# An adaLN transformer block with routed experts: token list built by one-hot matmuls, second expert row fetched by an accumulating transfer

## What is computed

```python
h = _layernorm(x) * (1 + ca) + sa
x = x + ga * linear_attention(h)            # 16 heads of 32, relu on q and k
h = _layernorm(x) * (1 + cb) + sb
x = x + gb * ffn(h)

# ffn: X is 4096 x 512, 8 experts, 2 per token
scores = sigmoid(X @ gate_w.T)
_, idx = top_k(scores + router_bias, 2)
w = scores[idx] / sum(scores[idx])
y_e = (silu(X @ W1[e]) * (X @ W3[e])) @ W2[e]        # inner width 352
out = sum_k w_k * y_idx_k + (silu(X @ sw1.T) * (X @ sw3.T)) @ sw2.T   # shared, width 704
```

## Time and profile before

| | |
|---|---|
| median of 3 runs | 1439.48 us |
| profiled execution | 1446.23 us, span 1444.4 us |
| mean granted TensorE clock | 0.934 |
| TensorE busy | 1249.8 us (87%) |
| VectorE busy | 661.2 us (46%) |
| GpSimd busy | 479.6 us (33%) |
| ScalarE busy | 415.7 us (29%) |

### The profile page before, as it was taken

The page is one execution under the profiler, slowest core; times in us unless marked ns, Lnnn a source line. Parts: engine busy times, 40 slices in busy tenths (PEclk is TensorE's granted clock), DMA queues, the critical chain, the costliest instruction groups (busy, mean ns, idle before and its releaser), DMA issues.

```text
span 1444.4 us, 25152 instructions
## 1 busy us (share of the span) xinstructions
PE 1249.8 (87%) x8990; PEld 788.6 (55%) x8990; DVE 661.2 (46%) x1376; ACT 415.7 (29%) x869; POOL 479.6 (33%) x460
## 2 busy tenths in 40 slices
PE   6997998998997989662488699999999999988896
PEld 2645665665665556440256456556565666565563
DVE  4555777777866556551145311111111111145764
ACT  2432443434433324230133212222222222211121
POOL 1213555555643322067400101111111111067661
PEclk9998999999998999885599899999999999989998
DMA  5724786987878577142135345655556555477773
GB/s 183 226 44 116 171 196 162 210 213 168 204 190 239 148 193 206 55 110 63 50 114 151 116 105 129 134 127 139 133 132 132 132 132 132 110 235 231 214 237 118
DMA packets 270067, 220.33 MB, mean 153 GB/s; under 512 B 190640, under 2 KB 203184, under 8 KB 269436
## 3 DMA queue, kind: packets, MB, share of 16 engines
q1 hardware_dynamic: 242424, 159.65, 43.8%
q0 software_dynamic: 12848, 35.47, 9.3%
q10 hardware_dynamic: 14680, 23.62, 5.7%
HBM read 117.29 MB, written 57.61 MB: 121 GB/s over the span
## 4 chain that ended last, share of the span: by engine, by line
PE 52%; issue 13%; DVE 10%; DMA 10%; POOL 9%; ACT 3%; SPq 3%; ACTq 1%; DVEq 0%; POOLq 0%
PE ps_o L75 6%; PE ps_vs L75 5%; PE ps_o L76 5%; PE ps_o L77 5%; PE ps_vs L76 5%; PE ps_vs L77 5%; DMA xt<-g 4%; PE ps_kh L75 2%; PE ps_kh L76 2%; PE ps_kh L77 2%; POOL ol L394 2%; DMA wp_raw<-in_wproj_t 2%; POOL h L381 1%; POOL xg L389 1%; PE ps_qh L75 1%
## 5 line engine op out<-in xcount | busy, mean ns | idle before, releaser
L455 POOL DMA_INDIRECT g<-h_d,slot_tab x71 | 67.1, 945 | 472.4 <-DMA xt<-g 352.1
L75 PE MATMUL ps_o<-w_all,xt 128*128 x568 | 179.6, 316 | 19.4 <-DMA xt<-g 19.3
L76 PE MATMUL ps_o<-w_all,xt 128*128 x568 | 179.5, 316 | 0.0
L77 PE MATMUL ps_o<-w_all,xt 128*128 x568 | 179.2, 316 | 0.0
L861 DVE SCALAR_TENSOR_TENSOR a<-ps_o,a 128x352 f32<-128x352 f32 x71 | 37.2, 524 | 183.3 <-PE ps_o L77 183.3
L866 DVE TENSOR_TENSOR at<-ps_y,at 128x384 f16<-128x384 f32 x71 | 39.6, 557 | 176.3 <-ACT at L1105 176.3
L75 PE MATMUL ps_kh<-s_ht,sh 128*128 128x256 f16 x256 | 79.5, 310 | 43.3 <-DVE s_act L620 30.4
L1110 ACT ACTIVATE y<-ps_vs,slot_tab 128x512 f32<-128x512 f32 x71 | 48.8, 687 | 230.5 <-PE ps_vs L77 230.5
L75 PE MATMUL ps_qh<-ht,wqkv 128*128 128x128 f16 x512 | 90.4, 223 | 2.5 <-DVE wqkv L613 2.5
L370 POOL TENSOR_TENSOR h<-cen,rows_f 128x512 f32<-128x512 f32 x32 | 40.6, 1268 | 154.4 <-ACT cen L904 143.0
L76 PE MATMUL ps_qh<-ht,wqkv 128*128 128x128 f16 x512 | 90.4, 223 | 0.0
(11 more groups left out here) (225 smaller groups left out, 3267.5 us busy)
## 6 DMA issues: line engine op xcount, KB each, us to landing
y_d<-y SPq DMA_DIRECT2D x71, 256.0 KB, 3.4
w_stage<-in_w_d ACTq DMA_DIRECT2D x64, 176.0 KB
xb<-in_x SPq DMA_DIRECT2D x32, 256.0 KB, 3.3
xr<-in_x SPq DMA_DIRECT2D x32, 256.0 KB, 4.2
x_d<-x SPq DMA_DIRECT2D x32, 256.0 KB, 3.5
h_d<-hl SPq DMA_DIRECT2D x32, 256.0 KB, 2.7
h2t_d<-h2t SPq DMA_DIRECT2D x32, 256.0 KB, 3.7
s_ht<-h2t_d SPq DMA_DIRECT2D x32, 256.0 KB
```

Of the source, the lines that this page charges most:

```text
L75: nc.tensor.matmul(out, lh, rh, start=first, stop=False, skip_group_check=True)
L76: nc.tensor.matmul(out, lh, rl, start=False, stop=False, skip_group_check=True)
L77: return nc.tensor.matmul(out, ll, rh, start=False, stop=last, skip_group_check=True)
L455: pool.indirect_dma_start(m.g[:, t % 2, :], None, m.h2_d, bass.IndirectOffsetOnAxis(ap=m.slot_tab[:, t, 0:1], axis=0)).then_inc(m.gathered ...
```

## The change

**Choosing.** `find_top` and `find_index` are replaced by `pick`: for each of the two ranks a maximum over all tiles at once, a comparison, and the lowest expert number of those equal. `add_runs` uses one scan in place of eight. The routing is done in steps 22 to 25.

**The list.** No table in DRAM. A token's slot is split into lane (slot mod 128) and tile (slot / 128). For each of 64 pairs of token tile and rank, VectorE makes two one-hot operands: `lane_is` (128x128) and `tile_is` (128 x 71 x 4), the latter times four values: tile number, token in the tile, and high and low part of the weight. TensorE adds up their products in one PSUM bank. Six pairs per step in steps 26 to 36; at step 37 `list_tokens` turns the sum into token numbers and weights.

**Weights.** From piece 22 on the low part is GpSimd's. As its subtraction can't scale, ScalarE scales the staged piece in place in a second pass. The 66 pieces are spread evenly over the steps up to the experts.

**Order.** EARLY is 8: the early stage is steps 22 to 47, and 48 steps run after the experts. **Combine.** `y_sum` is gone; the second row of a token is fetched with `compute_op=ALU.add` onto the first, once that has landed, three tiles ahead. GpSimd's constants grow by a few small instructions. The names of routing now take the room of the last two experts, so ScalarE waits for `listed` at piece 66.

```diff
-EARLY = 10
+EARLY = 8
...
+PAIRS = TOP * TILES
+PAIR_RING = 8
+PAIRS_PER_STEP = 6
+PAIRS_FROM = TAIL_STEPS + 4
+PICKED = 4
...
-    first = TAIL_STEPS + 2 * (q - TAIL_STEPS)
-    return range(min(first, E * WP), min(first + 2, E * WP))
+    left, steps, i = E * WP - TAIL_STEPS, EARLY_STEPS - TAIL_STEPS, q - TAIL_STEPS
+    return range(TAIL_STEPS + left * i // steps, TAIL_STEPS + left * (i + 1) // steps)
...
+def pair_turn(q):
+    first = PAIRS_PER_STEP * (q - PAIRS_FROM)
+    return range(min(max(first, 0), PAIRS), min(max(first + PAIRS_PER_STEP, 0), PAIRS))
...
-    for j in range(2):
-        sp.wait_ge(m.scattered[j], 16 * TILES)
-    sp.dma_start(m.slot_tab[:, :, :], m.table.rearrange("(p t) o -> p t o", p=P)).then_inc(m.table_loaded, 16)
...
-    pool.wait_ge(m.slots_ready, 1)
-    pool.wait_ge(m.table_stored, 16)
-    for t in range(TILES):
-        for k in range(TOP):
-            pool.indirect_dma_start(m.table, bass.IndirectOffsetOnAxis(ap=m.entry[:, k, t:t + 1], axis=0),
-                                    m.tab_src[:, k, t, :], None).then_inc(m.scattered[k], 16)
...
+    def w_low(p):
+        _, dst, rows, cols = w_piece(m, p)
+        pool.wait_ge(m.w_hi, p + 1)
+        pool.wait_ge(m.w_scaled, p - TAIL_STEPS + 1)
+        pool.tensor_tensor(dst[:, 1, :], m.w_stage[0:rows, p % W_RING, 0:cols], dst[:, 0, :], ALU.subtract).then_inc(m.w_lo, 1)
+
+    pool.wait_ge(m.w_lo, TAIL_STEPS)
+    for p in range(TAIL_STEPS, E * WP):
+        w_low(p)
...
     def fetch(i):
         if i < len(order):
             r = i % YB
+            at_least(pool, m.y_loaded[i % Y_RING], 32 * (i // Y_RING))
             if i >= YB:
                 before = order[i - YB]
                 pool.wait_ge(m.c_added if before < 2 * EARLY else m.s_t1_done, before + 1)
-            for k in range(TOP):
-                pool.indirect_dma_start(m.yb[:, r, k, :], None, m.y_d,
-                                        bass.IndirectOffsetOnAxis(ap=m.slot[:, k, order[i]:order[i] + 1], axis=0)).then_inc(m.y_loaded[i % Y_RING], 16)
-
-    def y_sum(i):
+            pool.indirect_dma_start(m.yb[:, r, 0, :], None, m.y_d,
+                                    bass.IndirectOffsetOnAxis(ap=m.slot[:, 0, order[i]:order[i] + 1], axis=0)).then_inc(m.y_loaded[i % Y_RING], 16)
+
+    def fetch_onto(i):
         r = i % YB
-        pool.wait_ge(m.y_loaded[i % Y_RING], 2 * ring_use(i, Y_RING))
-        pool.tensor_tensor(m.yb[:, r, 0, :], m.yb[:, r, 0, :], m.yb[:, r, 1, :], ALU.add).then_inc(m.y_summed, 1)
-
-    for i in range(2):
+        pool.wait_ge(m.y_loaded[i % Y_RING], 2 * ring_use(i, Y_RING) - 16)
+        pool.indirect_dma_start(m.yb[:, r, 0, :], None, m.y_d,
+                                bass.IndirectOffsetOnAxis(ap=m.slot[:, 1, order[i]:order[i] + 1], axis=0),
+                                compute_op=ALU.add).then_inc(m.y_loaded[i % Y_RING], 16)
+
+    for i in range(3):
         fetch(i)
     for i in range(len(order)):
-        fetch(i + 2)
-        y_sum(i)
+        fetch_onto(i)
+        fetch(i + 3)
...
+    def pick():
         v.wait_ge(m.scores_ready, 1)
+        v.wait_ge(m.r_consts, PICKED)
         step(v.tensor_tensor(m.sel[:, :, :], m.scores[:, :, :], m.bias[:, :].unsqueeze(1).to_broadcast([P, TILES, E]), ALU.add))
-        for t in range(TILES):
-            v.max(m.top[:, t, :], m.sel[:, t, :]).then_inc(m.r_step, 1)
-        steps += TILES
-        v.wait_ge(m.r_step, steps)
-
-    def find_index():
-        nonlocal steps
-        for t in range(TILES):
-            v.max_index(m.index[:, t, :], m.top[:, t, :], m.sel[:, t, :]).then_inc(m.r_step, 1)
-        steps += TILES
-        v.wait_ge(m.r_step, steps)
+        for k in range(TOP):
+            step(v.reduce_max(m.best[:, :], m.sel[:, :, :], AX.X))
+            step(v.tensor_tensor(m.cand[:, :, :], m.sel[:, :, :], m.best[:, :].unsqueeze(2).to_broadcast([P, TILES, E]), ALU.is_equal))
+            step(v.scalar_tensor_tensor(out=m.cand[:, :, :], in0=m.cand[:, :, :], scalar=-float(E),
+                                        in1=m.expert_far[:, :].unsqueeze(1).to_broadcast([P, TILES, E]), op0=ALU.mult, op1=ALU.add))
+            step(v.tensor_reduce(m.best[:, :], m.cand[:, :, :], AX.X, ALU.min))
+            step(v.tensor_tensor(m.choice[:, k, :, :], m.expert_no[:, :].unsqueeze(1).to_broadcast([P, TILES, E]),
+                                 m.best[:, :].unsqueeze(2).to_broadcast([P, TILES, E]), ALU.is_equal))
+            if k == 0:
+                step(v.scalar_tensor_tensor(out=m.sel[:, :, :], in0=m.choice[:, k, :, :], scalar=-BIG, in1=m.sel[:, :, :],
+                                            op0=ALU.mult, op1=ALU.add))
+        v.tensor_tensor(m.both[:, :, :], m.choice[:, 0, :, :], m.choice[:, 1, :, :], ALU.add).then_inc(m.both_ready, 1)
...
+    def pair(n):
+        t, k, r = n // TOP, n % TOP, n % PAIR_RING
+        at_least(v, m.pair_used, n - PAIR_RING + 1)
+        v.tensor_scalar(m.lane_is[:, r, :], m.lane_no[:, :], m.part[:, 0, k, t:t + 1], None, ALU.is_equal).then_inc(m.pair_ready, 1)
+        v.scalar_tensor_tensor(out=m.tile_is[:, r, :, :], in0=m.tile_no[:, :, :], scalar=m.part[:, 1, k, t:t + 1],
+                               in1=m.values[:, k, t, :].unsqueeze(1).to_broadcast([P, SLOT_TILES, 4]),
+                               op0=ALU.is_equal, op1=ALU.mult).then_inc(m.pair_ready, 1)
...
+    def list_tokens():
+        v.wait_ge(m.pair_used, PAIRS)
+        step(v.tensor_copy(m.listing[:, :, :], m.ps_list))
+        step(v.scalar_tensor_tensor(out=m.tokenf[:, :], in0=m.listing[:, :, 0], scalar=float(P), in1=m.listing[:, :, 1],
+                                    op0=ALU.mult, op1=ALU.add))
+        step(v.tensor_copy(m.slot_token[:, :], m.tokenf[:, :]))
+        step(v.tensor_tensor(m.tokenf[:, :], m.listing[:, :, 2], m.listing[:, :, 3], ALU.add))
+        v.tensor_scalar(m.slot_weight[:, :], m.tokenf[:, :], 1.0 / SCALE ** 2, None, ALU.mult).then_inc(m.listed, 1)
...
-    beside = {TAIL_STEPS: (find_top,), TAIL_STEPS + 1: (find_index,), TAIL_STEPS + 2: (weigh,),
-              TAIL_STEPS + 3: (add_runs,), TAIL_STEPS + 4: (place,), TAIL_STEPS + 5: (name_tiles,)}
+        step(v.tensor_copy(m.eid[:, :], m.eidf[:, :]))
+
+    beside = {TAIL_STEPS: (pick,), TAIL_STEPS + 1: (weigh,), TAIL_STEPS + 2: (add_runs,), TAIL_STEPS + 3: (place, name_tiles)}
     sum_logits()
     for q in range(TAIL_STEPS, EARLY_STEPS):
         multiply(q)
+        for n in pair_turn(q):
+            pair(n)
         low(q - 1)
         for work in beside.get(q, ()):
             work()
         if down_due(q):
             add(q // SH_TILES - 1)
-        for p in w_turn(q):
-            w_low(p)
+        if q == LIST_STEP:
+            list_tokens()
...
         act.wait_ge(m.w_loaded[p % W_RING], ring_use(p, W_RING))
-        act.activation(dst[:, 0, :], m.w_stage[0:rows, p % W_RING, 0:cols], ACT.Copy, scale=SCALE).then_inc(m.w_hi, 1)
+        staged = m.w_stage[0:rows, p % W_RING, 0:cols]
+        act.activation(dst[:, 0, :], staged, ACT.Copy, scale=SCALE).then_inc(m.w_hi, 1)
+        if p >= TAIL_STEPS:
+            act.wait_ge(m.w_hi, p + 1)
+            act.activation(staged, staged, ACT.Copy, scale=SCALE).then_inc(m.w_scaled, 1)
...
-        if q == TAIL_STEPS + 3:
+        if q == TAIL_STEPS + 1:
...
+        for n in pair_turn(q):
+            pe.wait_ge(m.pair_ready, 2 * n + 2)
+            nc.tensor.matmul(m.ps_list.rearrange("p t n -> p (t n)"), m.lane_is[:, n % PAIR_RING, :], m.tile_is[:, n % PAIR_RING, :, :].rearrange("p t n -> p (t n)"),
+                             start=n == 0, stop=n == PAIRS - 1, skip_group_check=True).then_inc(m.pair_used, 1)
```

More of the change, by code:

```diff
@@ L408, in gpsimd_program @@
         if s == 0:
-            step(pool.memset(m.zero[:, :], 0))
             step(pool.memset(m.ident[:, :], 0.0))
@@ L412, in gpsimd_program @@
                                     base=0, pattern=[[-1, P]], channel_multiplier=1))
-            step(pool.iota(m.token[:, :], [[P, TILES]], base=0, channel_multiplier=1))
-            step(pool.tensor_copy(m.tab_src[:, :, :, 0], m.token[:, :].unsqueeze(1).to_broadcast([P, TOP, TILES])))
         if s == 2:
@@ L639, in add @@
             v.wait_ge(m.sy_done, i + 1)
-            if n < EARLY and n in (0, 8):
-                v.wait_ge(m.s_gb_loaded, 48 if n == 0 else 64)
+            if n == 0:
+                v.wait_ge(m.s_gb_loaded, 48)
             v.wait_ge(m.act_done, SH_TILES * (n + 1))
@@ L782, in find_index @@
-    def find_index():
-        nonlocal steps
-        for t in range(TILES):
-            v.max_index(m.index[:, t, :], m.top[:, t, :], m.sel[:, t, :]).then_inc(m.r_step, 1)
-        steps += TILES
-        v.wait_ge(m.r_step, steps)
-    def weigh():
-        v.wait_ge(m.r_consts, 4)
-        for k in range(TOP):
-            step(v.tensor_copy(m.indexf[:, k, :], m.index[:, :, k]))
-            step(v.tensor_tensor(m.choice[:, k, :, :], m.expert_no[:, :].unsqueeze(1).to_broadcast([P, TILES, E]),
```

(17 more changed lines are left out.)

107 lines of the change are left out of this document (58 added, 49 removed).

## The result

The changed kernel takes 1473.85 us (median of four runs, 1473.1 to 1477.98). The kernel before, run beside it, takes 1438.87 us (four runs, 1435.37 to 1442.59). The ratio is 1.0249 with an interval of 1.0216 to 1.0281: slower by 35 us. The forecast was 1473.0, from 1430 to 1510.

The account below looks back on a forecast made before the run. It took weight pieces to pace undisturbed early chunks, beside a scatter stall; TensorE bounds the experts. From 1446.2 us, -11 before the experts and +45 in the combine stage gave 1480, less 6.7 for the median 1473; range 1430 to 1510.

Parts of the forecast that it names:

- the 14 for the clock: Early stage after 606 us: 14 us added for slower matmuls, an eighth to a half of 47 us being 6 to 24.
- Step 1: Early stage, 648.8 to 710.6 us: the 64 table scatters and the stall beside them go, -55.6 us.
- Rival B: Early stage: something other than the scatters holds the engines, so the stall stays, +55.6 us, 1529; chance 0.06.
- Step 2: Routing: fewer instructions save some 3 us; the down product of step 26 releases ScalarE at 606 instead of 609.1.
- Step 3: Weight pieces from 22 on: ScalarE's second pass and GpSimd's subtraction in series, 2.41 us narrow, 3.02 wide.
- Step 4: Steps 26 to 36: pairs take TensorE's lead, 7.7 us a step; first two chunks 60.4 and 53.6 us.
- Step 5: Combine stage: two more chunks add 53.4 us, less 4.5 and 4 from dropping GpSimd's sums; net +45.
- full relief: Combine stage: the lower bound of the net cost of moving twelve steps there, +39 us.
- Step 6: Combine stage: 32 accumulating transfers replace 32 sums; 0 us for the first tile.
- Rival C: Combine stage: accumulating transfers above 6.7 us each outlast a chunk; at 8 us, about 1505; chance 0.08.
- A: Steps 26 to 36: pairs cost TensorE no lead, pieces alone set the pace; 1434 to 1440 us; chance 0.15.
- D: Early stage: half of A, pair step near 6.5 us, pieces 2.4, first expert matmul near 783; 1440; chance 0.09.

Follow-up runs that it names:

- x6: Kernel before with the accumulating fetch and each residual row tile of the combine stage loaded one turn later: 1425.48 us, ratio 0.9903.
- x3: Kernel after with weight low parts back on VectorE, no second ScalarE pass, and TensorE's pair matmuls one step later: 1421.95 us, ratio 0.988.
- x4: Kernel after with ten chunks ahead of the experts instead of eight: 1474.17 us, ratio 1.0238 to the kernel before.
- x5: Kernel after with low parts on VectorE, pair matmuls one step later and ten chunks ahead of the experts: 1412.66 us, ratio 0.98.
- b1: The kernel before, unchanged, run on the second chip: 1385.63 us.
- e8: Kernel before with only the accumulating fetch, no sum on GpSimd: 1382.41 us, ratio 0.9974.
- e4: Kernel after with the weights' low parts back on VectorE and without ScalarE's second pass: 1447.45 us, ratio 1.0421 to the kernel before.
- e3: Kernel after with the plain second gather and GpSimd's sum back in the combine stage: 1493.36 us, ratio 1.0749 to the kernel before.
- e7: Kernel after with TensorE's pair matmuls one step later, behind up(q) and ahead of the down product: 1442.23 us, ratio 1.039 to the kernel before.

## Why the forecast held, step by step

The mechanisms were right in the main; that the time was right to a microsecond is luck. The first expert matmul came 11 us later than forecast (826.55 against 801.6 and the 14 for the clock), the combine stage was 14 us shorter (209.0 against 223), and the expert stage 2 us shorter. The last 6 us come from the step between the profiled execution and the median: the prediction took off 6.7 us, as in the kernel before, and in the kernel after it is 0.6 (1474.41 against 1473.85).

**Step 1, the stall goes (-55.6): right where the stall exists.** In the first measurement and on the third chip the traced programs with scatters (the kernel before, x6) have the stretch; those without (the kernel after, x3, x4, x5) don't: between 600 and 820 us no matmul of the kernel after waits for "issue". The size fits too: the kernel before differs by 1441.89 - 1385.63 = 56 us between a chip with it and one without, while the kernel after moves by 2. But it was read as what scatters do, and on the second chip b1 and e8 show 64 scatters at the same rate with TensorE at 16 to 18 of 20 us. On the first chip there is only the time of the kernel before, 1386.35. Nor is TensorE held all the while they are issued: they begin at 620.6, and from 635.3 to 648.8 eleven pass beside matmuls at full pace (TensorE busy for 13.04 of 13.50 us, granted clock 1.00). No run leaves out the scatters alone on a chip with the stall, so that they cause it stays likely and not shown. The forecast is therefore one for a chip with the stall: without it the same change costs 1.0629 instead of 1.0249. Rival B was wrong where the stall was seen. Beside 16 scatters in 20 us TensorE did 133 matmuls in b1, and 16 and 18 in the first trace and in x6. What differs between the chips no run shows.

**Step 2, choosing: right.** The down product released ScalarE at 605.79; the forecast said 606.

**Step 3, the third hand: right.** Forecast 2.41 and 3.02 us a piece. In the timeline of the kernel after, inside one step:
```profile
748.44 0.50 ACT L1044 ACTIVATE w_all<-w_stage 128x352 f16<-128x352 f32 x1
748.96 0.50 ACT L1047 ACTIVATE w_stage<-w_stage 128x352 f32<-128x352 f32 x1
749.60 0.85 POOL L457 TENSOR_TENSOR w_all<-w_stage,w_all 128x352 f16<-128x352 f32 x1 [12.36 <-ACT w_stage L1047]
750.87 0.50 ACT L1044 ACTIVATE w_all<-w_stage 128x352 f16<-128x352 f32 x1 [1.41 <-POOL w_all L457]
```
From rounding to rounding it is 2.43, with a subtraction of 0.85 (0.87 taken); the wide subtractions that start at 654.07 and 657.06 are 2.99 apart. The range leaves out the upper end of the piece bounds; no run shows such a bound, only these intervals. The plain chunk took 39.8 against 41.8, the last pieces 30.7 against 32.8.

**Step 4, the pairs take TensorE's lead: the mechanism right, the pairs priced too low.** The two chunks with pairs took 76.9 and 65.4 us against 60.4 and 53.6, or 28.3 more, of which the 14 us set aside for the clock cover half. With the 4 us of the last two chunks, 28.3 - 4 - 14 = 10 us is the error up to the last piece; gather and transpose took 8 us instead of 7. Two terms of a step can be seen in one step of VectorE's timeline in the kernel after:
```profile
625.46 0.28 DVE L849 TENSOR_SCALAR lane_is<-lane_no,part 128x128 f16<-128x128 f32 x1
625.65 0.51 DVE L850 SCALAR_TENSOR_TENSOR tile_is<-tile_no,part,values 128x284 f16<-128x284 f32 x1
...
626.70 0.87 DVE L849 TENSOR_SCALAR lane_is<-lane_no,part 128x128 f16<-128x128 f32 x1
627.49 0.50 DVE L850 SCALAR_TENSOR_TENSOR tile_is<-tile_no,part,values 128x284 f16<-128x284 f32 x1
...
629.96 0.50 DVE L850 SCALAR_TENSOR_TENSOR tile_is<-tile_no,part,values 128x284 f16<-128x284 f32 x1
630.38 0.41 DVE L645 TENSOR_TENSOR s_at<-s_act,s_at 128x256 f16<-128x256 f32 x1
```
First term: six pairs take 625.46 to 630.46, 5.0 us, not 3.8. Over the ten steps with six pairs it is 3.8 to 5.3, 4.6 in the mean, so 8 us in all. Without GpSimd's subtractions, in e4 and x3, it is 3.8 each time: 0.62 a pair, not 0.55, and the collisions add 0.8 a step, not 0.5. The compare takes 0.28 us, but 0.87 to 1.20 in 10 of 64 cases, each time with a subtraction of GpSimd already running. Where GpSimd has no piece to subtract, in x3, it never does (the last of the three is the longest, in ns):
```profile
L839 DVE TENSOR_SCALAR lane_is<-lane_no,part x64: 269/277/281, 617.4 to 706.6; 128x128 f16<-128x128 f32 x64
```
and in the kernel after:
```profile
L849 DVE TENSOR_SCALAR lane_is<-lane_no,part x64: 269/276/1198, 614.9 to 732.8; 128x128 f16<-128x128 f32 x64
```
The prediction looked for this at the two-input half of the pair, where it stood only 3 times in 64 (1.12 to 1.40 instead of 0.50), and it mostly stood at the one-input compare. GpSimd can be the one held, too: one subtraction took 3.86 us instead of 0.85 beside four pairs, whose compares took 0.27 each. One row of either kind:
```profile
645.93 3.86 POOL L457 TENSOR_TENSOR w_all<-w_stage,w_all 128x352 f16<-128x352 f32 x1 [5.72 <-ACT w_stage L1047]
657.14 1.40 DVE L850 SCALAR_TENSOR_TENSOR tile_is<-tile_no,part,values 128x284 f16<-128x284 f32 x1
```
The longest compare, at 616.09, took 1.20 us, beside a subtraction of 1.15 that had started at 616.05. Why it is mostly the compare that is stretched, no run shows.
Second term: from the last pair to the next activation 4.5 us pass, not 3.1, of which the up product was put at 2.6. That was 24 matmuls 0.11 apart, as where the granted clock is 1.00; the granted clock in this stretch (606 to 738 us) is 0.69. In TensorE's timeline the matmuls of the up product behind these pairs are 0.21 apart from 630.73 to 633.50 and 0.11 apart from 633.67 on; the ten up products of steps 27 to 36 take 41.6 us, where 0.11 throughout gives 23.6 and the prediction 26. Those 15.6 us about use up the 14 kept for the clock, so the error of 10 lies in the pairs (8) and in what is left over, which is not traced further. No run shows the eighth and the half of 47 us between which the 14 were taken; the runs show these 15.6 us in their place, and 23.93 us of busy time against 22.29 for the same 168 matmuls at a granted clock of 0.94 and of 1.00. The upper bound was too high as well: with busy time in inverse proportion to the granted clock, an estimate from these two chunks, the 0.74 of 592 to 609 makes work about a third longer, not half, some 16 and not 24 us more on 47.

**Step 5, twelve steps behind the experts (+45): mis-sized.** 209.0 instead of 223. The two chunks added 2 x 23.5 = 47 us instead of 53.4, and the six others fell by 15.9 (177.9 + 47 - 209.0), where 8.5 had been taken. A steady chunk fell by 3.2 us, where 0.8 had been taken: TensorE's idle time in it by 1.6 (26.70 - 23.93 to 23.50 - 22.29) and its busy time, for the same 168 matmuls, by 1.6. The latter is the clock, which went from 0.94 to 1.00 once GpSimd's sums no longer stretched VectorE's instructions (2.28 us, at most 0.69 for the same instruction in the kernel after); the prediction had no term for it. e3, with the sum back, measures the relief at 16 to 18 us. +31 lies 8 us beyond +39, which had been called full relief; its own terms, 53.4 - 4.5 - 8, give 41. And x4 shows that the move itself cost nothing net on this kernel: undone, it gives 36 us behind and takes 34.5 ahead of the experts. The premise that they were moved from a place where they were meant as cover holds only in part: ten steps with pairs take 105.8 us with 1.7 pieces a step and 113.0 with 2.5.

**Step 6, the accumulating transfer (0): nearly right.** It costs the first tile 4.5 us:
```profile
DVE yb L910 <- DMA yb<-y_d,slot: 13.6, 1, 13.6
```
against 9.1, and in the steady chunks no engine but GpSimd itself waits for such a transfer. Rival C was wrong.

Rivals A and D needed steps with pairs near 6.5 us apart; they are 10 apart, and even with both limits eased (x5) 7.3.

## What to carry to other kernels

A matmul that waits for small work of another engine costs more than its own time: it takes the lead of everything queued behind it. Put it behind the work that the other engines wait for (e7: 33 us for moving four lines), and work out a step as the round trip through all queues, at the clock that the thin stretch will have (0.69 here, from 606 to 738 us). Move an operation off an engine only after asking with whom it will then share: the low parts on GpSimd cost 28 us, the sum off GpSimd gained 18 in this kernel, and in the kernel before 4 until SyncE's load was moved too (e8, x6). And when a stretch shows "issue" gaps between matmuls that nothing in the program holds, run the kernel before on another chip ahead of pricing it: 56 of the 1439 us were such a gap, and the sign of a fix can hang on it (x3 is 0.988 of the kernel before where the gap is; its 1421.95 us stand against 1386 where it isn't).
